# Third attention's weights loaded during the last part of the quantised stage, and two folds begun ahead of the phase's end signal

## The reference, cut to what matters

```python
x = x + _L0_xattn_ref(_layernorm(x), ctx_768, ...)   # 16 heads, mask
x = x + _L0_ffn_ref(_layernorm(x), ...)              # silu
x = x + _L1_xattn_ref(_layernorm(x), ctx_768, ...)   # 8 heads
x = x + _L1_ffn_ref(_layernorm(x), ...)              # quantised, two layers
x = x + _L2_xattn_ref(_layernorm(x), ctx_768, ...)   # 16 heads
x = x + _L2_ffn_ref(...); x = x + _L3_xattn_ref(...); x = x + _L3_ffn_ref(...)

def _L2_xattn_ref(x, context, Wq, Wk, Wv, Wo, bo):   # L1 is the same with 8 heads
    q, k, v = x @ Wq, context @ Wk, context @ Wv     # split into heads of 64
    attn = softmax(q @ k.T * 64 ** -0.5)
    return (attn @ v) @ Wo + bo

def _L1_ffn_ref(x, W1, b1, W2, b2):                  # _qlinear quantises x (its own range) and W
    return _qlinear(gelu(_qlinear(x, W1, b1)), W2, b2)
```

## Time and profile before

| | before |
|---|---|
| median of three runs | 2473.2 us (2466.31 to 2475.54) |
| the profiled execution's own time | 2470.2 us |
| its span in the trace | 2468.4 us |
| PE busy | 2274.7 us, 92% |
| DVE busy | 1852.0 us, 75% |
| ACT busy | 1497.6 us, 61% |
| POOL busy | 523.1 us, 21% |
| the chain that ended last | PE 74%, DVE 12%, ACT 6%, issue 5% |

### The profile page before, as it was taken

The page is one execution under the profiler, slowest core; times in us unless marked ns, Lnnn a source line. Parts: engine busy times, 40 slices in busy tenths (PEclk is TensorE's granted clock), DMA queues, the critical chain, the costliest instruction groups (busy, mean ns, idle before and its releaser), DMA issues.

```text
span 2468.4 us, 49178 instructions
## 1 busy us (share of the span) xinstructions
PE 2274.7 (92%) x14859; PEld 1953.7 (79%) x14861; DVE 1852.0 (75%) x4361; ACT 1497.6 (61%) x3089; POOL 523.1 (21%) x734
## 2 busy tenths in 40 slices
PE   7899999999899899995478999999997999979998
PEld 6788888888688788873257888888886787879998
DVE  3778778877966788887964878878878666766666
ACT  6455565555354677777876666666664654636665
POOL 2022122221212112210001111111102442422333
PEclk8999999999999999997558999999999999989999
DMA  8344444445200444440014554555442000114445
GB/s 222 105 135 118 135 133 133 134 121 151 74 16 10 129 133 125 134 118 17 0 36 130 137 153 135 144 138 143 131 137 71 1 1 3 36 52 137 136 136 154
DMA packets 461643, 256.56 MB, mean 104 GB/s; under 512 B 25664, under 2 KB 442332, under 8 KB 461532
## 3 DMA queue, kind: packets, MB, share of 16 engines
q1 hardware_dynamic: 461532, 255.27, 37.5%
HBM read 150.10 MB, written 105.12 MB: 103 GB/s over the span
## 4 chain that ended last, share of the span: by engine, by line
PE 74%; DVE 12%; ACT 6%; issue 5%; DVEq 1%; DMA 0%; POOL 0%; ACTq 0%; SPq 0%; POOLq 0%
PE ps_o L903 12%; PE ps_s L887 11%; PE ps_p L87 7%; PE ps_p L89 6%; PE ps_p L88 6%; PE ps_t L876 6%; PE ps_o L1385 3%; PE ps_t L1385 2%; DVE a_e L1156 2%; PE ps_s L87 2%; DVE a_sm L1148 2%; PE ps_t L3013 2%; PE ps_o L3013 2%; ACT a_keys L1009 2%; PE ps_s L88 2%
## 5 line engine op out<-in xcount | busy, mean ns | idle before, releaser
L903 PEld LDWEIGHTS ps_o<-a_val,a_pt 128*128 128x128 f32 (+2 forms) x3200 | 413.1, 192 | 34.9 <-issue 9.1
L887 PE MATMUL ps_s<-a_keys,a_zt 128*128 128x308 f32 (+1 forms) x1024 | 418.1, 492 | 17.6 <-ACT a_keys L1009 9.8
L903 PE MATMUL ps_o<-a_val,a_pt 128*128 128x128 f32 (+2 forms) x3200 | 423.7, 276 | 6.8 <-ACT a_pt L1046 4.0
L1148 DVE TENSOR_REDUCE a_sm<-a_e 128x16 f32<-128x1232 f32 (+1 forms) x192 | 234.4, 1221 | 229.5 <-ACT a_e L1054 229.4
L1018 ACT ACTIVATE a_stage<-ps_p 128x512 f32<-128x512 f32 (+1 forms) x370 | 220.9, 597 | 286.8 <-PE ps_p L89 284.6
L1046 ACT ACTIVATE a_pt<-ps_t 128x512 f32<-128x512 f32 (+1 forms) x448 | 225.3, 505 | 162.0 <-PE ps_t L876 161.6
L1009 ACT ACTIVATE a_keys<-ps_p 128x308 f32<-128x308 f32 x603 | 257.2, 427 | 101.3 <-PE ps_p L89 100.9
L876 PE MATMUL ps_t<-ident,a_e 128*128 128x128 f32 (+1 forms) x1600 | 262.6, 277 | 33.1 <-DVE a_e L1156 30.9
L1137 DVE TENSOR_REDUCE a_mx<-ps_s 128x6 f32<-128x462 f32 (+1 forms) x512 | 255.7, 548 | 47.1 <-PE ps_s L887 29.3
L87 PE MATMUL ps_p<-ct_hi,a_mt_hi 96*128 (+1 forms) x603 | 258.9, 429 | 0.0
L1140 DVE TENSOR_TENSOR a_e<-ps_s,a_mx 128x462 f32<-128x462 f32 (+1 forms) x512 | 253.7, 545 | 0.0
(11 more groups left out here) (433 smaller groups left out, 4658.7 us busy)
## 6 DMA issues: line engine op xcount, KB each, us to landing
a_vals<-a_stage SPq DMA_DIRECT2D x160, 512.0 KB, 3.5
a_val<-a_vals SPq DMA_DIRECT2D x128, 576.0 KB
f_w<-in_L_ffn_W_dram SPq DMA_DIRECT2D x129, 256.0 KB, 2.6
a_vals<-a_stage SPq DMA_DIRECT2D x40, 416.0 KB
a_val<-a_vals SPq DMA_DIRECT2D x64, 256.0 KB
a_val<-a_vals SPq DMA_DIRECT2D x128, 40.0 KB
x<-in_x_dram SPq DMA_DIRECT2D x8, 512.0 KB, 6.9
out_dram<-x SPq DMA_DIRECT2D x7, 512.0 KB, 6.0
```

Of the source, the lines that this page charges most:

```text
L887: mm = eng.matmul(o, zt, keys[:, h0:h0 + nh, :], start=True, stop=not self.masked)
L903: mm = eng.matmul(c.ps_o[:, (i % 2) * P:(i % 2 + 1) * P], self.pt[0:r, n, :], self.val[0:r, i % 2, n, :], start=(n == 0), stop=(n == self. ...
L1148: eng.tensor_reduce(self.sm[:, :], e, AX.X, ALU.add).then_inc(st.sem, 1)
```

## The change

1. `early` becomes a list of claims to wait for instead of one semaphore. For the second attention it is the same wait as before. For the third it is new: `QuantFfn.places_read`, ten groups turned into integers by ScalarE and ten by VectorE. Then its SyncE part issues the eight weight transfers, waits for `before`, and goes on as before with the bias and the transfers for the next phase.
2. In `tensor`, the fold of the second and third attention comes ahead of the wait for `before`. In the second attention a wait for `added` of the phase in front, 15 of 16 groups, stands ahead of it. Inside the fold, the products of the pair with number 1, the first that write `ps_p`, wait for `before`.
3. In `scalar`, the fold comes ahead of the wait for `before` as well. `vector` and `gpsimd` are as they were.

```diff
@@ sync
         if not self.setup:
-            free = self.early or self.before
-            eng.wait_ge(free.sem, free.at(1))
+            for claim, n in self.early:
+                eng.wait_ge(claim.sem, claim.at(n))
             self.load_weights(eng)
@@
-            if self.early:
+            if not self.setup:
                 eng.wait_ge(self.before.sem, self.before.at(1))
             eng.dma_start(self.bias[:, :], ...)
@@ fold_tensor, products(p)
             eng.wait_ge(self.wt_ready.sem, self.wt_ready.at(p + 1))
+            if p == 1 and not self.setup:
+                eng.wait_ge(self.before.sem, self.before.at(1))
@@ tensor
+        if not self.setup:
+            if self.banks_free:
+                claim, n = self.banks_free
+                eng.wait_ge(claim.sem, claim.at(n))
+            self.fold_tensor(eng)
         eng.wait_ge(self.before.sem, self.before.at(1))
-        if not self.setup:
-            self.fold_tensor(eng)
@@ scalar
-        eng.wait_ge(self.before.sem, self.before.at(1))
         if not self.setup:
             self.fold_scalar(eng)
+        eng.wait_ge(self.before.sem, self.before.at(1))
@@ QuantFfn
+        self.places_read = [(self.low_ready, 10), (self.high_ready, 10)]
@@ build_phases
-            tail=name == "L2", early=phases[-1].before if name == "L1" else None,
-            known=phases[-1].next_stats if name == "L1" else None)
+            tail=name == "L2", early=[(ahead.before, 1)] if name == "L1" else ahead.places_read,
+            known=ahead.next_stats if name == "L1" else None,
+            banks_free=(ahead.added, GROUPS - 1) if name == "L1" else None)
```

More of the change, by code:

```diff
@@ L592, in __init__ @@
     def __init__(self, core, name, heads, wq, wk, wv, wo, bo, before, twice=False,
-                 gamma=None, beta=None, mask=None, setup=None, tail=False, early=None, known=None):
+                 gamma=None, beta=None, mask=None, setup=None, tail=False, early=None, known=None,
+                 banks_free=None):
         self.core, self.name, self.heads, self.before = core, name, heads, before
-        self.early, self.left, self.quant = early, None, None
+        self.early, self.left, self.quant = early or (), None, None
+        self.banks_free = banks_free
         self.setup = setup
@@ L3328, in build_phases @@
     for name, heads in (("L1", 8), ("L2", 16)):
+        ahead = phases[-1]
         add(CrossAttention, "a" + name[1], heads, *(i[f"{name}_xattn_{w}"] for w in ("Wq", "Wk", "Wv", "Wo", "bo")),
-            tail=name == "L2", early=phases[-1].before if name == "L1" else None,
-            known=phases[-1].next_stats if name == "L1" else None)
+            tail=name == "L2", early=[(ahead.before, 1)] if name == "L1" else ahead.places_read,
+            known=ahead.next_stats if name == "L1" else None,
+            banks_free=(ahead.added, GROUPS - 1) if name == "L1" else None)
         if name == "L1":
```

## The result

| | before | changed |
|---|---|---|
| median | 2475.54 us (2466.31 to 2478.39, 7 runs) | 2460.45 us (2456.76 to 2462.69, 7 runs) |
| the profiled execution | 2470.2 us | 2461.15 us |
| its span | 2468.4 us | 2459.3 us |

The ratio is 0.994, with an interval from 0.993 to 0.995. In two further comparisons (experiments 5 and 12) the changed kernel stood at 0.9955 [0.9942, 0.9969] and 0.9953 [0.9935, 0.997] against the kernel before. So the change wins 15 us in the first comparison and 11 to 12 in the other two, where 8.6 were forecast. The time lies in the range (2457 to 2471), in its fast half.

The account below looks back on a forecast made before the run. TensorE, busy 92% of the span, and phase handovers were taken as the bound. Terms 8.26 + 0.83 - 0.1 - 0.4 = 8.6 us gave 2473.2 - 8.6 = 2464.6, rounded to 2464.5 us, with 8 in 10 from 2457 to 2471.

Parts of the forecast that it names:

- The load gap, 8.26 us: End of quantised stage to third attention's fold: early weights and fold ahead of the signal start TensorE 8.26 us earlier.
- the mechanism of the fold: Third attention's fold: still 15.94 us from first transpose to first projection, at clock 0.50 as before.
- its own signs of being wrong: Signs included a signal wait at the fold, ScalarE's output-stage lines growing, or fold pairs 1.2 us apart instead of 1.83.
- the bounds of 6.6 and 11.1 us: Lowest and highest total gain from the summed terms, around the expected 8.6 us.
- The second attention's handover, 0.83 us: End of silu stage: the second attention's fold starts 0.83 us earlier without the signal wait; at least 0.6 gained.
- Bytes beside the output stage, 0.1 us: Weight transfers beside the quantised output stage slow ScalarE, costing 0.1 us, kept between 0 and 0.7.
- What else might be late: Third fold's other waits, second pair's products, VectorE, ScalarE and GpSimd, are early enough and cost nothing.
- The rival in which a wait takes the place of the old one: Third attention's handover: another wait takes half the gap, or stored values don't move along; 4 us left, 2469 us; 13%.
- late weights: Third attention: weights not there in time or change without effect; only 0.83 us won, 2472.4 us; 2%.
- the clock that stays low in the projections: Third attention's projections: the clock's rise doesn't come, some 20 us more, 2484 us; 3%.
- The granted clock, -0.4 us: Third attention's projections: the clock's rise moves relative to their start, a 0.4 us loss, kept from -2.0 to +1.6.
- the first rival: Third attention's fold itself gets the full clock: 4.4 us won there, 2.0 in projections; total 15.4 us, 2458 us; 6%.

Follow-up runs that it names:

- experiment 5: The changed kernel once more, as partner of three other runs: 2462.85 us, ratio 0.9955 against the kernel before.
- experiment 12: The changed kernel again, as partner of three later runs: 2462.04 us, ratio 0.9953 against the kernel before.
- experiment 1: Changed kernel, but every attention except the third waits for the end signal before its fold: 2463.89 us, ratio 0.9952 against before.
- experiment 3: Changed kernel with the third attention's weights early, but both folds waiting for the end signal: 2463.35 us, ratio 0.9958 against before.
- experiment 2: Changed kernel with only the second attention's fold ahead of the signal; third attention loads and folds as before: 2472.7 us, ratio 1.0 against before.
- experiment 6: Changed kernel with TensorE waiting for GpSimd's context copies ahead of the third fold, a 3.57 us pause: 2470.15 us, ratio 0.9979 against before.
- experiment 7: Both folds ahead of the signal, third attention's weights late, 50 identity matmuls ahead of the third fold: 2469.1 us, ratio 0.9982 against before.
- experiment 10: Changed kernel with TensorE waiting for GpSimd's copies ahead of the third fold, 12 identity matmuls before that wait: 2465.6 us, ratio 0.9966 against before.
- experiment 8: Changed kernel with 26 identity matmuls ahead of the first attention's fold at the program's start: 2459.87 us, ratio 0.9948 against before.
- experiment 4: Changed kernel with both folds ahead of the signal, but the third attention's weights loaded behind it: 2472.0 us, ratio 0.9991 against before.
- experiment 9: Changed kernel with 11 identity matmuls ahead of the first attention's fold at the program's start: 2457.63 us, ratio 0.9936 against before.

## Why the prediction was right, and where it was not

The time lay in the range, and the largest term, the gap, was right; the mechanism of the fold was not. One of its own signs of being wrong came: the fold's pairs stand 1.04 to 1.2 us apart instead of 1.83. That the profiled execution, forecast at 2461.6 us, took 2461.15 is luck: the clock won 5.2 us in the third attention, where a loss of 0.4 was forecast, and against that stand 3.7 us lost ahead of the change and 1.6 in the second attention. One sum is off as well: the bounds of 6.6 and 11.1 us, with 3 us added, give 2459 to 2470 and not 2458 to 2470.

**The load gap, 8.26 us: right.** Issues 16 us ahead of the fold, and the transfer of `Wo` gone from the chain. From the last output matmul to the first transpose TensorE no longer stands at all.

**The second attention's handover, 0.83 us: right in kind.** From silu's last matmul to the first projection it gave 7.35 - 6.22 = 1.1 us; experiments 1 and 3, where that fold still waits, keep 7.34. The medians of experiment 2 don't show it (ratio 1.0).

**Bytes beside the output stage, 0.1 us: right, it was nothing.** ScalarE's integers (L2036) over the groups of 1255 to 1270, in the view of that line's instructions (duration in ns: shortest, median, longest):

```profile
L2036 ACT ACTIVATE f_h<-f_h,ln_stats x5: 1133/1134/1134, 1256.4 to 1268.6; 128x1024 bf16 x5
```

against 1132 in the groups ahead of the transfers, and the whole stage has the length it had. (The eight transfers are two each of 256, 192, 192 and 256 KB, 1.84 MB rather than the 1.79 of the prediction, which changes nothing.)

**What else might be late: right.** No wait for the signal shows at L939. GpSimd's wait for nothing visible is 6.82 us long here, not 10.41, and its deviations at 1290.23 are in time. The rival in which a wait takes the place of the old one did not come, nor did that of late weights, nor the clock that stays low in the projections. The argument against the first of these, that all engines go on within 0.03 us of the signal, is not what the earlier trace rows show: they show TensorE alone, 0.07 us behind the signal at 796.47.

**The granted clock, -0.4 us: this term was mis-sized, and the first rival is what happened.** It measured +4.8 us in the fold (15.94 to 11.15) and +0.4 in the projections. The step that failed is "15.94 us of fold as before, at the clock as before". It rested on the earlier trace rows, a fold that is busy 8.00 of 8.00 us and stays at 0.50, and I read from it that the fold's own work can't bring the rise. That row is a fold with 8 idle us ahead of it, and the change takes away just that condition. A row of a fold without it was at hand: the second attention's, 0.83 us behind the silu stage, with four products in 0.47 us. I used it for the rival's price and not for its chance, 6%. It is not quite the same case, for the clock was up before that fold and it only had to stay so:

```profile
780.00:797.00 17.00, 16.16 (x125) 15.06 (x124) 8.02 (x36) 5.13 (x8) 3.62 (x6) 1.00 0.00 1
```

With experiments 6, 7 and 10 the condition is shown from both sides: a pause put in takes the full clock away though the weights are early, and a pause filled keeps it, with early weights and with late ones. And the rise doesn't need the fold: in experiment 6 it came in the pause, and in the nine executions without one it came 0.1 to 1.3 us behind the last output matmul.

The rule that I weighed points the right way. The Trainium skill, page "TensorE: Matmul & The Clock Gate", Part 1, section "What's actually happening", says that the throttled clock is the default and that activity releases it; I wrote that the trace of this fold doesn't bear it out. For the nine executions in which the third fold follows work, the traces agree with it: the full clock is there 1.5 us into the fold at the latest. They also show what it leaves open, since in experiment 6 TensorE is busy with the same fold for 12.86 of 13.00 us and the clock stays at its lower level.

**The rival's size: 15.4 us, measured 11 to 15.** Its 4.4 us for the fold were 4.8. Its 2.0 us more for the projections are what the kernels without a fall show (26.98 - 25.05 = 1.9 us, experiments 7 and 8), but mostly the clock falls at the fold's end, and then 0.4 are left, or 1.2 are lost (28.15). In the second attention such a fall costs 1.6 us (14.54 instead of 12.98). These falls, and an execution's luck at its start, differ by as much as the comparisons do (11 to 15 us); that they are the reason is not shown, since one execution of each kernel was profiled.

**Against the bound.** I gave 0.2 to faster by over 0.5%, 0.77 to within it. The first comparison has 0.6%, the other two 0.45 and 0.47%: the gain lies about at the bound.

**What stays open.** Why this fold keeps a full clock once it has come but raises a low one late (6.7 us in, experiment 3; 14.2 us, experiment 6) or not at all (before, experiments 2 and 4). It wasn't tried with other shapes or sizes of matmul. Why the clock rose in the pause of experiment 6 but not in those of before and experiments 2 to 4, behind the same output stage, is open too. Nor is it shown what decides whether the clock falls at the fold's end.

## What to carry to other kernels

A wait on TensorE can cost more than its length: 8.3 us of waiting for weights cost 13.3 us here, because the fold behind it, small matmuls, then ran at the lower clock. When a change removes or adds such a wait, take the duration of what stands behind it from a place with the same idle time ahead, and look in the trace for one at either clock. Where the wait can't be removed, identity matmuls in its place can buy the clock for what follows: 4.4 us at this kernel's start with 11 that ended before the data came, 3.0 with 26 that put the fold off.

## What the runs showed of the hardware

- When the granted clock had risen for good went with the idle time ahead of the third fold: none, by 1.5 us into it (seven executions, and two with the wait filled); 0.90 us, after 6.7 us (one); 3.57 us, after 14.2 us (one; it had risen in the pause and fallen again); 8 us, not in the 16 us of the fold (three).
- At the very start of the program the granted clock reads 1.00 in every kernel, but the first fold's pairs come 1.84 us apart, as at 0.50 elsewhere, unless matmuls ran ahead of it. Transposes of the context behind it give another sign: 18 of them (L552) took 1.41 us in the profiled execution of before and 2.55 in that of the changed kernel, with the clock reading 1.00 in both. There the durations have to be read, not the clock.
- An identity matmul of 128x128 in 32 bits took 0.45 us at the pace of the low clock (11 in the 4.91 us of experiment 9's start) and 0.21 us at the full one (19, as 38 records, in the 4.00 us from 1282 of experiment 7).
- GpSimd's wait for nothing visible ahead of its deviations was 10.41 us in the kernel before and 6.82 us in the changed one. It is no fixed cost, and what it waited for isn't shown.
